# A two-layer graph network on one core: another instruction order in the steady bodies, and a first stage whose e_j is spread by TensorE

## What is computed

```python
h = maximum(layernorm(x), 0)                       # LN1
Wh = h @ W;  e = leaky(Wh @ a1 [:, None] + Wh @ a2 [None, :], 0.2)
attention = softmax(where(adj > 0, e, -9e15))
x = x + elu(attention @ Wh)
h = maximum(layernorm(x), 0)                       # LN2
A = (adj != 0)
for i in range(3):                                 # layers
    h = gru(A.T @ (h @ weight[i]), h)              # gates r, z, n
x = x + h
```

## Time and profile before

| | |
|---|---|
| median of three runs | 689.54 us |
| the profiled execution | 689.75 us, its span 687.9 us |
| busy: TensorE, DVE, ScalarE, POOL | 91%, 78%, 66%, 37% of the span |
| mean granted clock of TensorE | 0.984 |
| moved by DMA | 47.39 MB, 68 GB/s of HBM traffic over the span |
| first neighbours of batch 0 begin | 62.59 us |

### The profile page before, as it was taken

One profiled execution on the slowest core, in us unless ns is written; L12 is line 12 of the kernel. 1 busy time (PEld: TensorE's weight loads), 2 busy tenths in 40 slices (PEclk: granted clock), 3 DMA queues, 4 the chain that ended last, 5 costly groups with the idle time before them and its releaser, 6 DMA issues.

```text
span 687.9 us, 8791 instructions
## 1 busy us (share of the span) xinstructions
PE 623.6 (91%) x2845; PEld 458.4 (67%) x2845; DVE 539.0 (78%) x1234; ACT 451.9 (66%) x777; POOL 255.4 (37%) x263
## 2 busy tenths in 40 slices
PE   2686999998999899998999989998999999999995
PEld 2465776676686676776766766766767776767774
DVE  4767998599876998779985998769987699648545
ACT  2784787477874778566875778647785677554443
POOL 1203544246241461525432453414715234413440
PEclk9799899999999999999999999999999999999998
DMA  6521131023202132022410132021320122001001
GB/s 222 183 93 62 62 121 32 33 61 123 92 31 92 33 123 92 15 79 61 146 39 32 62 123 92 30 81 44 122 93 6 56 87 67 1 1 30 1 1 30
DMA packets 28669, 47.39 MB, mean 69 GB/s; under 512 B 1672, under 2 KB 19408, under 8 KB 28624
## 3 DMA queue, kind: packets, MB, share of 16 engines
q1 hardware_dynamic: 28624, 46.84, 21.0%
HBM read 42.60 MB, written 4.23 MB: 68 GB/s over the span
## 4 chain that ended last, share of the span: by engine, by line
PE 55%; DVE 26%; ACT 8%; issue 5%; POOL 5%; DMA 1%; DVEq 0%; ACTq 0%; POOLq 0%
PE ps_x L970 14%; PE ps_g L1008 10%; PE ps_x L951 6%; DVE score L665 5%; DVE zh L757 3%; ACT score L389 3%; PE ps_r L1017 2%; DVE zh L764 2%; PE ps_z L1018 2%; PE ps_z L1017 2%; PE ps_r L1019 2%; PE ps_r L1018 2%; PE ps_z L1019 2%; DVE hkT L751 2%; DVE nn L744 2%
## 5 line engine op out<-in xcount | busy, mean ns | idle before, releaser
L1008 PE MATMUL ps_g<-edges,h_hi 128*128 128x512 f32 x384 | 157.7, 411 | 10.6 <-DVE h_lo L773 9.2
L1008 PE MATMUL ps_g<-edges,h_lo 128*128 128x512 f32 x384 | 152.2, 396 | 0.0
L389 ACT ACTIVATE score<-score,nmax 128x1024 f32<-128x1024 f32 x64 | 73.8, 1153 | 48.1 <-DVE nmax L665 47.1
L970 PE MATMUL ps_x<-probT,h_nat 128*128 128x512 f32 x224 | 98.9, 594 | 0.0
L1008 PEld LDWEIGHTS ps_g<-edges,h_hi 128*128 128x128 f32 x384 | 73.1, 190 | 29.0 <-DVE h_lo L773 12.8
L665 DVE CUSTOM_DVE_ANT_0 score<-score,away 128x1024 f32<-128x1024 f32 x64 | 86.6, 1353 | 7.3 <-ACT score L383 6.5
L300 POOL TENSOR_SCALAR tz<-tz 128x512 f32<-128x512 f32 x32 | 24.6, 769 | 172.9 <-ACT tz L430 172.9
L275 POOL TENSOR_SCALAR rstd<-mv 128x4 f32<-128x4 f32 (+1 forms) x24 | 9.9, 412 | 199.4 <-DVE mv L707 146.9
L1008 PEld LDWEIGHTS ps_g<-edges,h_lo 128*128 128x128 f32 x384 | 73.2, 191 | 14.0
L396 ACT ACTIVATE probT<-ps_x 128x512 f32<-128x512 f32 x128 | 70.9, 595 | 17.2 <-PE ps_x L951 17.1
L951 PE MATMUL ps_x<-ident,score 128*128 128x128 f32 x512 | 71.0, 281 | 11.4 <-ACT score L389 10.0
(11 more groups left out here) (136 smaller groups left out, 1331.5 us busy)
## 6 DMA issues: line engine op xcount, KB each, us to landing
adj_in<-in_adj SPq DMA_DIRECT2D x64, 512.0 KB, 3.3
x_nat<-in_x SPq DMA_DIRECT2D x8, 512.0 KB, 4.3
ej<-ej_kept_at SPq DMA_DIRECT2D x8, 512.0 KB, 3.4
out<-nn SPq DMA_DIRECT2D x16, 256.0 KB, 2.3
probT<-in_L_gnn_weight SPq DMA_DIRECT2D x1, 192.0 KB
probT<-in_L_gnn_w_ih SPq DMA_DIRECT2D x1, 192.0 KB
probT<-in_L_gnn_w_hh SPq DMA_DIRECT2D x1, 192.0 KB
ej_kept_at<-ej_row SPq DMA_DIRECT2D x8, 4.0 KB
```

The lines of the kernel that those rows point to most:

```text
L389: act.activation(score[t % U][:], score[t % U][:], ACT.Exp, bias=nmax[:, t:t + 1], scale=-1.0, accum_out=rowsum[:, t:t + 1]).then_inc(exp_ ...
L970: last = pe.matmul(bank_of("agg", c, par)[:], h_nat[par][:, j, :], probT[:, j, :], start=(j == 0), stop=(j == T - 1))
L1008: last = pe.matmul(ps_g[c][:], part[:, s, :], edges[par][:, s, cols(c)], start=(s == 0 and part is h_hi), stop=(s == T - 1 and part is h_lo))
```

## The change

**Steady bodies.** TensorE: the first tile's transpositions stand before the return of the last state's half 1; the first h product waits for one output sum, z is formed before r there, and r waits for the second; the return of layer 0's half 0 stands ahead of the last product of `gates_g(b, 0, 1)`; the return of a half 1 stands in the middle of `neighbours(l, 0, 1)` instead of ahead of it. DVE: `g_lo_half(b, 0, 0)` stands right behind the first output sum; LN1 of batch b + 2 moves to layer 1 and its dot products to the end of the body; away tile 1 moves into the body before; in layer 0 the edge tiles move behind the new state, one of them ahead of `lo_half(b, 0, 1)`. ScalarE: exp of tile 1 moves behind hnb, h of batch b + 2 to the end of layer 1 and into layer 2. POOL: LN1's power moves into layer 1.

**First stage.** ScalarE's queue issues the weights, the four small loads first; x and LN1 of batch 0 go in halves; e_j of batches 0 and 1 is spread by TensorE (`wide_half`: a transposition of a column broadcast to 128 columns) and copied to `ej` by ScalarE; the other weights are transposed and copied later; DVE takes the second copy of tiles 2 to 7; the attention products go a tile at a time, 128 columns wide; h of batch 1 moves behind the tiles, LN2's power of half 1 ahead of POOL's split of half 0, and four edge tiles, the layers' products and their splits into the time around the first neighbours.

The core of the diff:

```diff
@@ tensor: first gates, g products, returns
-                if l == 0 and c == 0:
-                    pe.wait_ge(out_done, b * 2 + 1)
+                if l == 0 and c == 0 and b > 0:
+                    pe.wait_ge(out_done, b * 2)
...
+                if l == 0 and c == 0:
+                    product(ps_z[:], whh(1), h, True, False)
+                    if b > 0:
+                        pe.wait_ge(out_done, b * 2 + 1)
                 product(ps_r[:], whh(0), h, True, False)
...
                 product(ps_z[:], of_g(1), g, False, True).then_inc(z_ps, 1)
+                if l == 0 and c == 1:
+                    h_back(b, 0, 0)
...
                     neighbours(b, par, l, 0, 0)
+                    neighbours(b, par, l, 0, 1, range(0, TH // 2))
                     h_back(b, l - 1, 1)
-                    neighbours(b, par, l, 0, 1)
+                    neighbours(b, par, l, 0, 1, range(TH // 2, TH))
@@ tensor: first stage
+            def wide_half(b, c):
+                if b == 0:
+                    pe.wait_ge(first_ej, c + 1)
+                else:
+                    pe.wait_ge(e_done, b * 2 + 1)
+                    pe.wait_ge(setup_copy, 3)
+                for t in range(c * TH, (c + 1) * TH):
+                    last = pe.transpose(wide_bank(b, c)[:, tile_cols(t % TH)], ej_col[:, t:t + 1].broadcast_to([P, P]),
+                                        ident[:])
+                last.then_inc(wide_ps, 1)
...
+            def first_agg_tile(t, par=0):
+
+                for j in range(T):
+                    if j % TH == 0:
+                        pe.wait_ge(*prob_count(0, t, j // TH))
+                    last = pe.matmul(bank_of("agg", t // TH, 0, True)[:, tile_cols(t % TH)], h_nat[par][:, j, :],
+                                     probT[:, j, tile_cols(t % TH)], start=(j == 0), stop=(j == T - 1))
@@ vector: first stage and body
+            def first_probT(t):
+                dve.wait_ge(probT_ps, 2 * t + 2)
+                dve.tensor_copy(probT[:, TH:T, tile_cols(t % TH)],
+                                bank_of("probT", 2 * t + 1, 0, True)[:].rearrange("p (j i) -> p j i", j=TH)
+                                ).then_inc(probT_dve, 1)
...
                     out_half(b - 1, a_par, 0)
-                if attend:
-                    away_tile(a, a_par, 1)
+                g_lo_half(b, 0, 0)
                 if b > 0:
                     out_half(b - 1, a_par, 1)
                 if attend:
                     scores(a, 1)
-                if prepare:
-                    norm1(b + 2, par)
-                g_lo_half(b, 0, 0)
                 g_lo_half(b, 0, 1)
...
                 n_input(b, 1, 0)
+                if prepare:
+                    norm1(b + 2, par)
                 new_h(b, 1, 0)
...
                 g_lo_half(b, 2, 1)
+                if prepare:
+                    dots_ej(b + 2)
                 if attend:
                     split_h0(a, 0)
                 if prepare:
+                    dots_ei(b + 2, par)
                     away_tile(b + 2, par, 0)
+                    away_tile(b + 2, par, 1)
@@ gpsimd
                 rstd2_half(0, 0)
+                rstd2_half(0, 1)
                 split_h(0, 0, 0)
-                rstd2_half(0, 1)
                 split_h(0, 0, 1)
```

More of the change, by code:

```diff
@@ L176, in bank_of, with prob_count, wide_bank, ln_count @@
                 return FIRST_BANK[kind, k]
+            if first and kind == "probT":
+                return ps_x[k % 2]
             n = JOB[kind, k]
             return ps_x[(n + par + JOBS[n][5]) % 2]
+        def prob_count(b, t, k):
+            if b == 0 and t >= 2:
+                return (probT_dve, t - 1) if k == 1 else (probT_done, t + 3)
+            return probT_done, 2 * (b * T + t) + k + 1 - (T - 2 if b > 0 else 0)
+        def wide_bank(b, c):
+            return ps_x[c] if b == 0 else (ps_hn, ps_r)[c]
+        def ln_count(b):
+            return b + 2 if b > 0 else 2
         def adj_count(b, t):
@@ L618, in setup_layer, with first_norm1 @@
                 dve.tensor_tensor(cT_lo[:, l, :], bk[:, 0:3 * F], cT_hi[:, l, :], ALU.subtract).then_inc(setup_dve, 1)
+            def first_norm1(c):
+                dve.wait_ge(x0_loaded[c], 16)
+                for t in range(c * TH, (c + 1) * TH):
+                    last = dve.bn_stats(stats[:, t, :], x_nat[0][:, t, :])
+                last.then_inc(stats_done, 1)
+                dve.wait_ge(stats_done, c + 1)
+                for t in range(c * TH, (c + 1) * TH):
+                    last = dve.bn_aggr(mv[:, t, :], stats[:, t, :])
+                last.then_inc(mv_done, 1)
@@ new lines, in first_dots @@
+            def first_dots(k, c, done):
+                dst = ej_col if k == 1 else ei[0]
+                for t in range(c * TH, (c + 1) * TH):
+                    last = dve.scalar_tensor_tensor(dot[:, k, t, :], h_nat[0][:, t, :], 1.0, w_rep[:, k, :], ALU.mult,
+                                                    ALU.mult, accum_out=dst[:, t:t + 1])
+                last.then_inc(*done)
+            def first_probT(t):
[3 more added lines that the diff above has]
+                                ).then_inc(probT_dve, 1)
@@ L801, in first @@
                 x1_half(0, 0, 1)
-                setup_layer(2)
+                dots_ei(1, 1)
+                for t in range(TA + 1, T):
+                    edge_tile(0, 0, t)
                 split_h0(0, 1, True)
                 away_tile(1, 1, 0)
+                setup_layer_lo(0)
+                setup_layer_lo(1)
+                setup_layer_lo(2)
+                away_tile(1, 1, 1)
             def body(b, par, attend, prepare):
@@ L942, in bank_free @@
                     if not isinstance(m, int) or -ahead <= m < B - ahead and not (m == 0 and (job, k) in FIRST_BANK):
-                        pe.wait_ge(s, (m + ahead) * per + count)
+                        if job == "probT" and m == 0:
+                            for half in range(2):
+                                pe.wait_ge(*prob_count(0, T - 1, half))
+                        elif job == "probT":
+                            pe.wait_ge(*prob_count(m, k // 2, k % 2))
+                        else:
+                            pe.wait_ge(s, (m + ahead) * per + count)
                         return
```

331 lines of the change are left out of this document (191 added, 140 removed).

## The result

The changed kernel takes **667.67 us** (median of four runs, 667.17 to 668.37) beside 689.53 for the kernel before (median of four). The ratio is 0.9681, with a 95% interval of 0.9664 to 0.9697: 21.9 us or 3.2% faster. The forecast was 666.5, its range 653 to 678. The profiled execution took 668.37 us, its span 666.6.

The account below looks back on a forecast made before the run. TensorE, busy 91% of the span, was taken as the bound. Gains 11.9 + 2.1 - 2.5 + 10.5 + 1.4 = 23.4, rounded to 23, off 689.54 gave 666.5 us, range 653 to 678.

Parts of the forecast that it names:

- First stage, 11.9 earlier: From the start to the first neighbours: these come at 50.7 us, 11.9 earlier, bounds 8 and 14.
- halves and early weights let h end about 3.0 us sooner: First stage, h of batch 0: loading x in halves and small weights first ends it about 3.0 us sooner.
- From the first neighbours to the end of the first sums, 2.1 earlier: Up to body 0's first sums: shorter h0 wait and full clock, less added products, net 2.1 us earlier, between 0 and 3.
- A steady body, 2.1 earlier: Bodies 1 to 5: reordering saves 2.1 us each, 10.5 for five; bounds 4.3 and 0 per body.
- The new late wait: Steady body, late neighbours: TensorE waits 2.0 us for h_lo of half 1, a price of the new order.
- The lead of 3.9: Steady body at layer 1's first neighbours: TensorE is 3.9 us ahead of the old order, before the late price.
- Body 0, 2.5 later: Body 0: meets the late wait (2.0) and 0.5 more at its start, so 2.5 us later (0 to 4).
- Bodies 6 and 7, 1.4 earlier: Last two bodies: body 6 saves 0.8 us and body 7 0.6, together 1.4 earlier.
- The steady order closes its idle time: Rival, steady bodies: POOL's split falls clear, late wait 0.5, a body saves 3.9; 655 us, chance 0.2.
- The late wait eats all: Rival, steady bodies: sum and away tile both stretched, or hkT's chain slips 1 us; saving 0, 677 us, chance 0.17.
- The loads interleave: Rival, first stage: batch 0's x lands 1 us later; 667.5 us, or 671 with that stage's lower bound; chance 0.1.
- The clock rival: Rival, first stage and bodies: longer waits bring half clock, 43 us lost for 23 won; 709 us, chance 0.03.

Follow-up runs that it names:

- f2: Changed kernel with ScalarE again making all sixteen copies of batch 0's transposed probabilities (VectorE made six): 669.21 us.
- f1: Changed kernel with e_j of batch 0 again transposed as one row, stored to memory and read back to all partitions: 672.34 us.
- b3: Changed kernel with POOL's split of the first state's half 0 (layer 1) held until VectorE has split half 1: 674.27 us.
- f4: Changed kernel with eight more products of batch 0, overwritten unread, where TensorE waits at 57 to 60 us: 666.74 us.
- b6: Changed kernel with the return of half 1 of a state at layer 1 back behind 8 instead of 12 products: 670.56 us.
- b5: Changed kernel with edge tile 2 back behind the split of half 1 (h_lo): 668.44 us.
- b2: Changed kernel with LN1's statistics of batch b + 2 and POOL's rstd again ahead of g_lo in bodies 1 to 5: 678.28 us.
- n1: Changed kernel with POOL's four splits made to wait for VectorE's work, edge tile 2 behind tile 3's scores, large weight loads behind x: 656.42 us.
- f3: Changed kernel with the three large weight loads issued only when both halves of batch 0's x have landed: 666.76 us.
- b7: Changed kernel with POOL splitting half 1 of the next batch's h0 only behind the last state's sum: 661.71 us.

## Why the prediction was right

The time was 1.2 us above the forecast, and the table of leads shows where terms went another way. The sum is nearer than its terms: misses of 2.4, 1.5 and 0.4 us stand against 1.2 and 1.1 the other way, so that part of its closeness is luck.

- **First stage, 11.9 earlier: measured 11.5, by two errors that cancel.** The step "halves and early weights let h end about 3.0 us sooner" failed: h ends at 11.01 where it ended at 12.61, 1.6 sooner. The profile after shows why: POOL takes 1.72 us for the rstd of a half (7.61 to 9.33) where it took 2.39 for the whole (7.01 to 9.40), so the second half's ends when the old one did, and only ScalarE's first half is won. Against it, the tiles' step was put too long: the 16 passes of 128 columns take 1.79 to the next instruction, not 2.1, so a tile takes 2.66, not 3.05. At the end of the last attention product the two have cancelled (46.33, predicted 46.3); from there to the first neighbours it took 4.7, not 4.4. ScalarE is in step with TensorE here: one more copy a tile makes the step 3.14 in f2. That the memory trip is wholly on the path is shown by f1.
- **From the first neighbours to the end of the first sums, 2.1 earlier: this term was wrong.** It came out 0.3 later (11.5 to 11.2). The clock fell all the same in this execution, and the wait was halved in its first place only to return as 1.30 in a second: behind POOL's rstd, ScalarE's h0 and a split on DVE stretched by POOL. So it lies just outside its bounds of 0 to 3, on the side that they give to a falling clock, and half clock beyond 30 us is what the prediction named as a sign of being wrong. b3 and f4 show that a full clock gives 1.6 back.
- **A steady body, 2.1 earlier: measured 2.3.** The old waits went as predicted or further (hkT 0.41 where 0.8 was expected, the output sum 0 where 0.25 was). The new late wait was predicted as 2.0 in one place and is 1.72 in two. One stretched operation was reckoned, at 1.1: it is not the away tile but the sum before it, by 0.97, with 0.4 on the edge tile beside it. The lead of 3.9 doesn't follow from the waits listed, which give 2.9 (0.45 + 0.02 + 1.58 + 0.85); measured they give 3.7. The 2.1 itself rests on the time of 251.9 for h_lo, given without its working: 1.9 earlier at the late neighbours, where 2.3 was measured. The further working was wrong in one point: the place of the return and the edge tile, to which the prediction put down most of the wait, win nothing when they are undone (b6, b5). And the ledger hid how the gain is spread: by b2, LN1's place alone is worth 2.1 of the 2.3.
- **Body 0, 2.5 later: 1.4** (11.2 to 9.8). **Bodies 6 and 7, 1.4 earlier: nothing won** (21.5 to 21.3); body 7's waits of 0.71, 0.87 and 0.48, behind DVE as in the steady body, took back what its start had won.

The rivals. "The steady order closes its idle time" gave 655 on the condition that POOL's split falls clear of DVE's sum and away tile. It didn't fall so by itself; made to do so, in n1 (with the edge tile and the large loads moved too), it gives 656.4 and a period of 76.8 where the rival had 76.5. By its own terms the rival should have had 76.8 and 657: 3.9 - 0.5 + 0.2 is 3.6 a body, not 3.9. "The late wait eats all" wasn't met, and its price was too high: one more stretch of 1.1 leaves 1.0 of a body's 2.1, so 672 and not 677. But b3 shows how near it is: POOL's first split placed 4 us later in the body cost 6.6 us. "The loads interleave" drew on the Trainium skill, "DMA: Bandwidth & Descriptors", section "Issuing engines are not separate DMA queues". With two queues issuing, the first half of x was there at 4.36 at the latest (the whole x at 4.51 before, with one queue), and at 3.97 with the large loads held back (f3), so its price isn't seen here. The clock rival didn't happen, but its mechanism did, in b6: two of the eight waits of some 2 us were followed by half clock, and none of 1.1.

## What to carry to other kernels

In an in-order queue, look for work that nobody waits for soon and that stands ahead of work that the bounding engine waits for: one such operation, 2.3 us long, was worth 2.1 us a body. Where VectorE and POOL work side by side, place POOL's operations beside VectorE operations that read PSUM, and not beside the SBUF operations of the critical chain; one added wait was worth 6 us (b7), but the same kind of move at another place cost 6.6 (b3). And what removing a wait brings can't be read from its row alone: 0.81 for 0.41 in b7, nothing for 0.15 in b5, where a wait of 0.14 came up elsewhere.

## What the runs showed of the hardware

- A DVE operation with all operands in SBUF, of the kinds seen here, begun beside POOL's hT_hi, hT_lo or zh, ends 0.53 to 0.55 behind POOL's end (sum 0.69 to 1.66, away tile 0.68 to 1.78, edge tile 0.68 to 1.10) or, where it is a score of 1.22, 1.1 behind (2.30). The other way round POOL waits for DVE: hT_hi, 0.62 alone, takes 0.81 to 1.70. DVE operations of 128x512 that read PSUM keep 0.66 to 0.69 beside POOL. The Trainium skill, "SBUF — State Buffer", section "SBUF: two separate sides", says that VectorE and GpSimd share a pair of ports as an exclusive lock, held for the whole instruction, and that a VectorE operation needs it in a two-port mode or with two SBUF inputs. The rows agree: the loser waits, it isn't slowed in proportion, and LN1's statistics, with one SBUF input, keep 0.27 to 0.28 each beside zh. One row differs: beside POOL's power for rstd `tr`, with two SBUF inputs, keeps its 0.69.
- POOL's four small operations for rstd, in the first stage, take 1.7 to 1.8 us for 4 columns and 2.4 for 8, so that two halves in a row take longer than the whole.
- A wait of 0.41 us on TensorE cost 0.81 from the transpositions ahead of it to the product behind it (2.04 beside 1.23), as the overlap with its neighbours is lost too.
